# First-tile weight sums of a fused attention and gated MLP kernel: taken from the ring's blocks, with no second load of the weights

## The reference

```python
xn = layernorm(x)
q, k, v = split(xn @ W_qkv.T + b_qkv)              # 16 heads of 16
q, k = elu(q) + 1, elu(k) + 1
att = (q @ (k.T @ v)) / clip(q @ sum(k), 1e-6)     # by head
att = layernorm(att @ W_proj.T + b_proj) * gamma + beta + xn
h = silu((xn @ w1.T) * s1) * ((xn @ w2.T) * s2)    # 256 -> 1024
h = gelu((h @ h1.T) * hs1)                         # 1024 -> 1024
h = gelu((h @ h2.T) * hs2)                         # 1024 -> 1024
out = x + att + (h @ w3.T) * s3                    # 1024 -> 256
```

## Time and profile before

| what | value |
|---|---|
| median of 3 runs | 1534.72 us |
| the profiled execution | 1534.54 us |
| its span, first to last instruction | 1532.4 us |
| mean granted clock of TensorE | 0.997 of full |
| PE busy | 1506.4 us, 98% |
| VectorE busy | 1144.8 us, 75% |
| ScalarE busy | 936.2 us, 61% |
| POOL busy | 465.8 us, 30% |
| DMA moved | 291.85 MB, 190 GB/s |

### The profile page before, as it was taken

How to read it: one execution, slowest core, us unless ns; L and a number is a source line. 1 busy time by engine, 2 the same in 40 slices (tenths; PEclk the granted TensorE clock), 3 DMA queues, 4 the chain that set the end, 5 groups by cost and what they waited for, 6 DMA issues and landing times.

```text
span 1532.4 us, 33225 instructions
## 1 busy us (share of the span) xinstructions
PE 1506.4 (98%) x11022; PEld 1419.7 (93%) x11022; DVE 1144.8 (75%) x2056; ACT 936.2 (61%) x1727; POOL 465.8 (30%) x555
## 2 busy tenths in 40 slices
PE   8989999999999999999999999999999999999998
PEld 6988999989999898998989999899998999989897
DVE  5646878678686877868778787786868778677786
ACT  4535756656566565656657566565765656666564
POOL 2022504224042341513425043240523405234140
PEclk9999999999999999999999999999999999999999
DMA  9898754818448284573737538275481845737364
GB/s 272 275 287 270 243 185 130 279 58 266 158 142 279 65 263 132 184 235 100 250 110 228 197 112 284 65 254 171 138 287 51 260 151 164 255 90 244 127 203 152
DMA packets 92417, 291.85 MB, mean 190 GB/s; under 512 B 7392, under 2 KB 52576, under 8 KB 69088
## 3 DMA queue, kind: packets, MB, share of 16 engines
q0 software_dynamic: 43296, 231.75, 46.3%
q1 hardware_dynamic: 48384, 58.62, 12.1%
q10 hardware_dynamic: 704, 1.05, 0.2%
HBM read 274.62 MB, written 23.07 MB: 194 GB/s over the span
## 4 chain that ended last, share of the span: by engine, by line
PE 87%; DVE 6%; DMA 3%; ACT 2%; issue 2%; DVEq 0%; POOL 0%; SPq 0%; ACTq 0%; POOLq 0%
PE ps L934 49%; PE ps L909 13%; PE ps L1007 8%; PE ps L812 4%; PE ps L813 4%; PE ps L814 4%; DMA weight_set<-in_w_ffn 2%; PE ps L854 2%; DVE values_a L1530 2%; PE ps L865 1%; PE ps L875 1%; PE ps L824 1%; DVE exp_tmp L1510 1%; DVE operands_a L1538 1%; ACT gate_ring L1168 1%
## 5 line engine op out<-in xcount | busy, mean ns | idle before, releaser
L934 PE MATMUL ps<-operands_a,hidden_weights 128*128 128x256 f32 x5040 | 644.9, 282 | 7.1 <-DVE operands_a L1538 7.1
L934 PEld LDWEIGHTS ps<-operands_a,hidden_weights 128*128 128x128 f32 x5040 | 615.1, 188 | 11.4 <-DVE operands_a L1538 10.1
L1571 DVE TENSOR_TENSOR partial_sums<-partial_sums,ps 128x512 f32<-128x512 f32 x300 | 204.2, 685 | 156.5 <-PE ps L934 106.8
L1538 DVE TENSOR_TENSOR operands_a<-values_a,operands_a 128x512 fp32r<-128x512 f32 x315 | 233.9, 762 | 34.1 <-POOL values_a L698 22.2
L706 POOL DMA_DIRECT2D hidden_weights<-weight_blocks x236 | 131.0, 555 | 402.3 <-PE ps L934 383.5
L909 PE MATMUL ps<-xnT,w_ffn 128*128 128x512 f32 x1024 | 253.0, 399 | 0.0
L934 PE MATMUL ps<-operands_b,hidden_weights 128*128 128x256 f32 x1680 | 234.9, 282 | 0.8 <-DVE partial_sums L1571 0.8
L909 PEld LDWEIGHTS ps<-xnT,w_ffn 128*128 128x128 f32 x1024 | 189.0, 188 | 41.9
L934 PEld LDWEIGHTS ps<-operands_b,hidden_weights 128*128 128x128 f32 x1680 | 213.6, 188 | 4.2 <-issue 3.0
L683 POOL TENSOR_TENSOR values_a<-values_a 128x512 f32<-128x512 f32 x30 | 38.3, 1276 | 340.7 <-DVE values_a L1530 340.7
L1233 ACT ACTIVATE values_out<-partial_sums,vectors 128x256 f32<-128x256 f32 x180 | 81.6, 501 | 94.9 <-DVE partial_sums L1571 94.9
(11 more groups left out here) (128 smaller groups left out, 2238.3 us busy)
## 6 DMA issues: line engine op xcount, KB each, us to landing
hidden_weights<-weight_blocks POOLq DMA_DIRECT2D x180, 1024.0 KB, 5.3
hidden_weights<-weight_blocks POOLq DMA_DIRECT2D x60, 512.0 KB, 4.2
raw_weights<-weight_blocks SPq DMA_DIRECT2D x48, 272.0 KB, 2.7
hidden_weights<-in_w_ffn POOLq DMA_DIRECT2D x16, 512.0 KB, 10.2
weight_set<-in_w_ffn SPq DMA_DIRECT2D x16, 512.0 KB, 10.6
weight_blocks<-weight_set SPq DMA_DIRECT2D x16, 512.0 KB, 2.8
out_dram<-acc SPq DMA_DIRECT2D x32, 256.0 KB, 2.2
x<-in_H SPq DMA_DIRECT2D x15, 512.0 KB, 5.6
```

The source lines that it names most:

```text
L934: r = mm(bank[:, m * HT:(m + 1) * HT], ring_weights[:, place, 2 * g + j, m * P:(m + 1) * P], as_used(buf[:, j, slot[block_of_b], part, :]) ...
L1538: v.tensor_tensor(lo_part(group, block), value(group, block), hi_part(group, block).bitcast(F32), ALU.subtract).then_inc(lo_half.sem, 1)
L1571: v.tensor_tensor(scratch[:, dst, :], scratch[:, kept, :], product_bank(s, i), ALU.add).then_inc(add.sem, 1)
```

## The change

- `load_set` and its four loads per set go, on SP and in the prologue.
- `sum_of_weights(i, n)` reads the ring's blocks of tile 0, and writes into one buffer `weight_sums` of four blocks for all sets, in the memory that sets 0 to 2 used. The order of calls is 0, 1, 2, 3. A sum waits for the blocks it reads, and for the store of the former set's sum out of its place.
- `first_block` waits, besides PE's product, until the sums that read the former block in the place are made (`READ_BY_SUM`).
- On POOL, three more blocks (A22 of set 2, A11 and A21 of set 3) go ahead of `ln1(1)`. `w_out` waits for the stored sums of set 3 instead of set 2, and so does `clear_low`; ScalarE's wait for the sums of set 3 goes.
- On VectorE, the first two sums of set 2 go ahead of two of H1's low parts.
- The raw block A21 of each set is copied to `weight_blocks` too (16 copies instead of 12), so that the check reads it: a check piece has 608 columns instead of 544.
- The second pass loads the sets again and makes its own sums.
- `WARM_UP` is 7 instead of 6.

```diff
-STAGE_ORDER = (A22, A11, A21, A12)
-SUM_FOR = (5, 6, 7, 3)
-SUM_ORDER = (0, 2, 1, 3)
-READ_BY_SUM = {0: 3, 1: 4}
+SUM_FOR = (5, 7, 6, 3)
+READ_BY_SUM = {A22: 1, A21: 2, A11: 3, A12: 4}
+SUM_READ_BY = {0: 3, 2: 4}
...
-WARM_UP = 6
-BLOCKS_PER_TILE = SETS * PRODUCTS * BLOCK_COLS // B
+WARM_UP = 7
+BLOCKS_PER_TILE = SETS * (PRODUCTS + 1) * BLOCK_COLS // B
...
-    stage = [sb(f"weight_set_{i}", [P, 4, HK, 2 * P], at=z_at if i < 3 else ha_at + pair_bytes + o_bytes)
-             for i in range(SETS)]
+    sums = sb("weight_sums", [P, 4, HK, 2 * P], at=z_at)
...
             def copy_blocks(i):
                 for product, b in RAW_OF.items():
                     dst = block_place(i, product).rearrange("p (j o) -> p j o", j=HK)
                     sp.dma_start(dst, hidden_block(i, b)).then_inc(s_copied[i], 16)
+                at = (SETS * PRODUCTS + i) * BLOCK_COLS
+                dst = blocks_dram[:, at:at + BLOCK_COLS].rearrange("p (j o) -> p j o", j=HK)
+                sp.dma_start(dst, hidden_block(i, A21)).then_inc(s_copied[i], 16)
...
             def first_body():
                 store_sums(0)
                 load_x(1, 0)
-                load_set(1)
                 store_sums(1)
-                load_set(2)
                 store_sums(2)
-                load_set(3)
                 store_sums(3)
...
             def first_block(set_, b):
                 if b in PLAIN_READ[set_]:
+                    of_set, old = next((i, o) for i in range(set_ - 1, -1, -1) for o in PLAIN_BLOCKS
+                                       if PLAIN_PLACE[i][o] == PLAIN_PLACE[set_][b])
+                    pool.wait_ge(s_sums[of_set], READ_BY_SUM[old])
                     step, n = PLAIN_READ[set_][b]
                     pool.wait_ge(*plain_prod.after(0, f"{step}{n}"))
...
             def first_body():
...
                 first_block(2, A12)
+                first_block(2, A22)
+                first_block(3, A11)
+                first_block(3, A21)
                 ln1(1)
                 inverse_root(0, 1, ln2_var, ln2_root)
-                first_block(2, A22)
-                for b in PLAIN_BLOCKS:
-                    first_block(3, b)
-                for at in range(4):
-                    pool.wait_ge(s_stored[2][at], 16)
-                for at in READ_BY_SUM:
-                    pool.wait_ge(s_sums[2], READ_BY_SUM[at])
+                first_block(3, A12)
+                first_block(3, A22)
+                for n in range(4):
+                    pool.wait_ge(s_stored[SETS - 1][n], 16)
+                pool.wait_ge(s_sums[SETS - 1], 4)
                 pool.dma_start(w_out[:], w_ffn[:, F_OUT:]).then_inc(s_w_out, 16)
...
                 transposed_hi(1, 1)
-                for at in range(4):
-                    act.wait_ge(s_stored[3][at], 16)
                 for c in ("C11", "C12", "C21", "C22"):
                     plain_gelu_of(3, c)
...
             def sum_of_weights(i, n):
+                a = {b: ring[:, PLAIN_PLACE[i][b]].bitcast(F32) for b in PLAIN_BLOCKS}
+                s1, s3, s2, s4 = (sums[:, k] for k in range(4))
+                if i > 0:
+                    dve.wait_ge(s_stored[i - 1][n], 16)
+                    if n in SUM_READ_BY:
+                        dve.wait_ge(s_sums[i - 1], SUM_READ_BY[n])
+                if n == 0:
+                    dve.wait_ge(s_first[i][A21], 16)
+                    dve.wait_ge(s_first[i][A22], 16)
+                    v.tensor_tensor(s1, a[A21], a[A22], ALU.add).then_inc(s_sums[i], 1)
+                elif n == 1:
+                    dve.wait_ge(s_first[i][A11], 16)
+                    v.tensor_tensor(s3, a[A11], a[A21], ALU.subtract).then_inc(s_sums[i], 1)
...
                     plain_lo_of("H1", "B11")
                     plain_lo_of("H1", "B12")
+                    sum_of_weights(2, 0)
+                    sum_of_weights(2, 1)
                     plain_lo_of("H1", "B21")
                     plain_lo_of("H1", "B22")
...
+                    sum_of_weights(2, 2)
                     sum_of_weights(2, 3)
...
```

More of the change, by code:

```diff
@@ L559, in load_piece @@
                     sp.dma_start(raw[:, n + GATE_PER_TILE:], of_out).then_inc(piece_loaded[j].sem, 16)
[L561 to L570, removed]
             def copy_blocks(i):
@@ L575, in copy_blocks, with store_sum, exact_sums @@
                     sp.dma_start(dst, hidden_block(i, b)).then_inc(s_copied[i], 16)
-            def store_sums(i):
[L578 to L581, removed]
+                at = (SETS * PRODUCTS + i) * BLOCK_COLS
+                dst = blocks_dram[:, at:at + BLOCK_COLS].rearrange("p (j o) -> p j o", j=HK)
+                sp.dma_start(dst, hidden_block(i, A21)).then_inc(s_copied[i], 16)
+            def store_sum(i, n):
+                src = sums[:, n].rearrange("p j o -> p (j o)")
+                return sp.dma_start(block_place(i, SUM_FOR[n]), src)
+            def store_sums(i):
+                for n in range(4):
+                    sp.wait_ge(s_sums[i], n + 1)
+                    store_sum(i, n).then_inc(s_stored[i][n], 16)
+            def exact_sums():
+                for i in range(SETS):
+                    if i > 0:
+                        sp.wait_ge(exact_stored.sem, exact_stored.at(i - 1, 3))
+                    for n, b in enumerate((A22, A21, A11, A12)):
+                        sp.dma_start(sums[:, n], hidden_block(i, b)).then_inc(exact_set.sem, 16)
+                    for n in range(4):
+                        sp.wait_ge(exact_sum.sem, exact_sum.at(i, n))
+                        store_sum(i, n).then_inc(exact_stored.sem, 16)
+                sp.wait_ge(exact_stored.sem, exact_stored.at(SETS - 1, 3))
             def store_out(t, first):
@@ L1636, in clear_low @@
             def clear_low():
-                for at in range(4):
-                    dve.wait_ge(s_stored[2][at], 16)
+                for n in range(4):
+                    dve.wait_ge(s_stored[SETS - 1][n], 16)
                 v.memset(low[:], 0).then_inc(s_low0, 1)
@@ new lines, in exact_sums @@
+            def exact_sums():
+                a22, a21, a11, a12 = (sums[:, k] for k in range(4))
+                for i in range(SETS):
+                    dve.wait_ge(exact_set.sem, exact_set.at(i, 3))
+                    v.tensor_tensor(a22, a21, a22, ALU.add).then_inc(exact_sum.sem, 1)
+                    v.tensor_tensor(a21, a11, a21, ALU.subtract).then_inc(exact_sum.sem, 1)
+                    dve.wait_ge(exact_sum.sem, exact_sum.at(i, 1))
+                    v.tensor_tensor(a11, a22, a11, ALU.subtract).then_inc(exact_sum.sem, 1)
+                    dve.wait_ge(exact_sum.sem, exact_sum.at(i, 2))
+                    v.tensor_tensor(a12, a12, a11, ALU.subtract).then_inc(exact_sum.sem, 1)
@@ L1928, in _, with second @@
             run(0)
-            second_pass_if_needed(dve, lambda: run(B))
+            def second():
+                exact_sums()
+                run(B)
+            second_pass_if_needed(dve, second)
 def kernel(**inputs):
```

49 lines of the change are left out of this document (22 added, 27 removed).

## The result

The changed kernel takes 1524.22 us (median of 4 runs, 1524.13 to 1524.34) against 1535.13 (median of 4, 1534.2 to 1536.57): 0.9928 of the time before, 95% interval 0.9916 to 0.994. That is 10.9 us less; 1523.6 was forecast, from 1522.4 to 1528.4. In a later comparison on one chip the change took 1523.52 (median of 5, 1522.85 to 1525.26) and the kernel before 1535.39 (median of 21), so 11.9 us less. The profiled execution took 1524.34 us, span 1522.5, mean granted clock 0.998.

What follows compares the result with a forecast made beforehand. PE was taken to bound the kernel (87% of the chain), with its recoverable losses in the first tile and at the start. 1534.54 - 9.5 - 1.4 = 1523.6 us, the other terms taken at nothing; range 1522.4 to 1528.4.

Steps and rivals of the forecast that it cites:

- Part 1: First tile: second load goes, sums read the ring; PE losses of 2.9 + 4.5 + 1.5 + 0.6 go, 9.5 us.
- The last 0.6: First tile, `plain_out_group(1)`: 0.6 us lost on ScalarE, regained by removing its wait for set 3's stores.
- The other two blocks ahead of `ln1(1)`: POOL, first tile: A11 and A21 of set 3 cost two issues and a wait until about 71.5; ScalarE doesn't notice.
- Part 2: `w_out` waits for set 3's last sum: landed at 107.7, wanted at 109.4; taken at nothing, 1.7 us of cover.
- rival C: PE stops for `w_out` ahead of `plain_out_group(1)`: 0.5 to 4.8 us more, 1524.1 to 1528.4; chance 0.19.
- Part 3: Small edits: copies end at 130 against 137.4; wider checks at most 84 ns each, 5.4 us of VectorE; taken at nothing.
- Part 4: Start: a seventh warm-up fills PE's first pause, full clock from 12 us; 1.4 us gained, bounds 1.4 and minus 0.6.
- A: The forecast itself: each stop has a named cause that disappears; 1523.6 us; chance 0.48.
- B: The start's clock gives nothing: 1525.0 us, with the delay 1525.6; chance 0.20.
- D: The wider checks lie on the path, a bit in each tile: up to 1529.0 us; chance 0.05.
- E: Waits moved, not removed: A22 of set 3 lands only at 102.6; about 1535 us, no change; chance 0.03.
- F: VectorE reading blocks PE loads weights from slows PE during the first tile's 16 sums; 1536.7 us at a third; chance 0.05.

Runs made afterwards that it cites:

- act_waits: The changed kernel with ScalarE again waiting for the stored sums of set 3 ahead of its first GELU of set 3: 1524.03 us, 0.9936 of the time before.
- ln1_first: The changed kernel with POOL's old order, `ln1(1)` and `inverse_root` ahead of the three moved blocks: 1526.32 us, 0.994 of the time before.
- after_warm6: The changed kernel with six warm-ups instead of seven: 1523.48 us, 0.9919 of the time before.
- before_warm7: The kernel before with seven warm-ups instead of six, nothing else: 1536.43 us, 1.0003 of the time before.
- after_again: The changed kernel itself, measured again as yardstick in a later comparison: 1523.52 us, 0.992 of the time before.
- narrow_check: The changed kernel without the four added copies of A21, check pieces 544 columns again: 1523.56 us, 0.9918 of the time before.
- bytes_kept: The changed kernel with SP again moving the 16 removed blocks, into a spare DRAM tensor nothing reads: 1526.94 us, 0.9939 of the time before.
- set3_late: The changed kernel with POOL loading A22 of set 3 only after the last product of step 2: 1532.0 us, 0.9979 of the time before.
- w_out_late: The changed kernel with `w_out` loaded only after the last product of step 3: 1533.36 us, 0.9985 of the time before.

## Why the prediction was right, and where it wasn't

- **Part 1, 9.5 us forecast, 9.8 in the profiled pair.** Term by term, forecast and measured: 2.9 and 3.0, 4.5 and 4.46, 1.5 and 1.63, 0.6 and 0.62. VectorE's dates came out one to three us earlier than the steps said, of which 1.2 are only the sooner start of the span (PE came to step 0's stop at 43.22, not 44.41): sums of set 1 from 52.54 (53.8 forecast), H1's first low part at 70.13 (about 72), sums of set 3 over at 91.1 (94.2), `transposed_lo` at 95.6 (97.5). The landing of A22 of set 3, for which I took the shortest of the earlier trace rows, 6.3, was 3.9; those 16 loads were measured in a kernel that also had the second load, and this one now goes with SP's queue empty.
- **The last 0.6, "which the last term needs"**: wrong in its reason. act_waits shows that the wait may stay. Once the sums are early, the wait ends before ScalarE comes to it; I should have compared 97.7, my own release, with the time of the first GELU.
- **"The other two blocks ahead of `ln1(1)`"**: right that step 2's second stop goes, wrong that this is what the move is for. In ln1_first step 2 has no stop, and 2.3 us are lost at `w_out`. The prediction followed POOL's order for what it delays and not for what VectorE then releases.
- **Part 2**: right. Issue at 96.47 (97.7 forecast), landing 9.0 us later (10.0), 2.6 us of cover (1.7); in the other profiles of the new first tile without a stop there, 1.1 to 2.8. The price of rival C was too small: its worst case, 4.8, had no slow clock in it, which added 2.4 and 2.7 us to stops of 5.3 and 7.3. That packets taken in turn leave `w_out` most of the bandwidth holds once the load moves (40 packets beside 39, 0.33 MB beside 0.04), but it would have had the load there in about half the time; the start of some 4 us behind SP's queue was in neither.
- **Part 3**: right. Checks +68 ns, under the bound of 84, and hidden; the copies ran from 91.5 to 124.5 us (94.3 to 130 forecast).
- **Part 4, 1.4 us**: not borne out by the time. The profiled pair does show 1.19 there: the 12 matmuls take 1.25 less (3.10 and not 2.91 at full clock), and one more warm-up puts the first projection off by 0.2 to 0.5 us. But neither run with the other number of warm-ups moved the median. The step that failed took the state of one profiled execution as that of all: six warm-ups kept the clock in after_warm6 and lost it in two other profiles. And the prediction didn't ask whether time gained at the start reaches the end: in the kernel before it doesn't, since a later load sets the moment (before_warm7).
- **Why the sum fits all the same.** In part by luck. In the profiled pair the start's 1.2 were given back by 1.5 of slow clock in the last tile. After that stop of 2 us the clock fell in seven profiled executions (the change, after_again, narrow_check, bytes_kept, ln1_first, set3_late, w_out_late: its 20 matmuls take 3.6 to 4.2 us) and not in five (after_warm6, act_waits, and all three with the old first tile: 2.6 us). Whether the change makes it more likely, and so pays this cost more often than the kernel before, stays open; an edit that would settle it wasn't tried. In the medians the change gained 10.9 and 11.9, and 12.3 without the seventh warm-up, more than Part 1's 9.5. Part of that is that the profiled execution of before was one of its better ones: 1534.54 against medians of 1535.1 to 1535.8. before_warm7 has the same first tile, with stops of 1.34, 2.28 and 3.96 us and the clock at 0.50 until past 118, and needs 111.28 us from step 0's stop to tile 1's (43.57 to 154.85), 10.8 more than the change; it had come to step 0's stop 0.84 sooner. That the rest is made of such differences is argued from these profiles and not shown.
- **Rivals.** A by its mechanism, with B's start. C is a real threshold 1 to 3 us away, and not crossed. D and E are out. F is out as well: while VectorE makes the sums of set 3, from 86.23 to 91.1, PE keeps its pace; the 160 matmuls around them take 18.94 us, 0.118 each as before.

## What to carry to other kernels

When an engine waits for a second copy of what is already on the chip, the gain is found by following its late releases through all engines in order, and counting PE from start to start. Then look at what the removed wait was covering: the next tight place here (`w_out`, 1 to 3 us away) is two links behind the edit, and a one-line change of order on POOL brings it on the path. A clock state that stands in one profile of one execution is no term of a sum; ask first whether a second profile of the same code has it, and whether a later wait would swallow what it gives.

## What the runs showed of the hardware that wasn't expected

- A 1024 KB load issued by POOL beside SP's DRAM to DRAM copies took 8.6 to 10.5 us in eleven profiles, though its bytes moved in some 4 us; no byte of it moved in about the first 4. The same start was seen with the issue at 106.05 (first bytes between 110 and 112).
- A 512 KB ring load took 3.9 us with SP's queue empty, 7.5 right behind another one (ln1_first), 8.3 beside SP's added copies (bytes_kept), and 6.3 to 19.6 in the kernel before.
- A stop of 5.3 or 7.3 us of PE cost 7.7 or 10.0, with a granted clock of 0.50 behind it; stops of 1.5 and 1.6 left it at 1.00. A stop of 2 us in the last tile was followed by 0.50 in seven profiled executions and by 1.00 in five.
- In the last tile a VectorE low part took 2.23 us, against 0.69 for the same part in tile 2. That is what makes the last tile's stop 2 us long instead of 0.38. In both tiles an operation of POOL's begins during it, after 0.4 us in the last tile (1449.23) and after 0.5 in tile 2 (236.71), so that VectorE was held up by POOL is likely and not shown:

```profile
1448.84 2.23 DVE L1546 TENSOR_TENSOR operands_a<-values_a,operands_a 128x512 fp32r<-128x512 f32 x1
```
